# Four attention tiles' sums transposed by VectorE instead of TensorE, in all batches in the same slot

## The reference, cut to what matters

```python
attn_in = jnp.tanh(jnp.einsum('bsd,da->bsa', hidden, W1) + b1)
scores = jnp.einsum('bsa,a->bs', attn_in, v)
mask = where(pt == 0, l <= j, where(pt == 1, l >= j, l != j))   # per batch
p = softmax(where(mask, scores[:, None, :], -1e30), axis=-1)
pooled = einsum('bjl,bld->bjd', p, hidden) / cnt
x = x + pooled
```

## Time and profile before

| what | value |
|---|---|
| median of 3 executions | 500.68 us |
| the profiled execution | 501.22 us |
| its span, first to last instruction | 499.4 us |
| granted TensorE clock, mean | 0.998 |
| PE busy | 493.0 us, 99% of the span |
| DVE busy | 348.8 us, 70% |
| ACT busy | 260.3 us, 52% |
| POOL busy | 236.0 us, 47% |

### The profile page before, as it was taken

The page is one execution under the profiler, slowest core; times in us unless marked ns, Lnnn a source line. Parts: engine busy times, 40 slices in busy tenths (PEclk is TensorE's granted clock), DMA queues, the critical chain, the costliest instruction groups (busy, mean ns, idle before and its releaser), DMA issues.

```text
span 499.4 us, 6992 instructions
## 1 busy us (share of the span) xinstructions
PE 493.0 (99%) x2320; PEld 407.7 (82%) x2320; DVE 348.8 (70%) x702; ACT 260.3 (52%) x506; POOL 236.0 (47%) x201
## 2 busy tenths in 40 slices
PE   8999999999999999999999999999999999999996
PEld 5787888888888888888888888888888888888985
DVE  5587235885688799786478689788568779644467
ACT  4655555543457574444446656454345757445243
POOL 1575446445264446444544447444525444746023
PEclk9999999999999999999999999999999999999999
DMA  5865354322255443422227454422222342331002
GB/s 154 185 185 150 101 147 147 100 85 85 85 120 145 116 115 87 127 85 84 85 85 169 123 161 123 132 84 85 85 85 85 100 112 84 88 131 37 0 1 84
DMA packets 77657, 52.97 MB, mean 106 GB/s; under 512 B 40758, under 2 KB 67382, under 8 KB 77622
## 3 DMA queue, kind: packets, MB, share of 16 engines
q1 hardware_dynamic: 75734, 50.44, 35.5%
q10 hardware_dynamic: 1888, 2.10, 1.3%
HBM read 48.33 MB, written 2.10 MB: 101 GB/s over the span
## 4 chain that ended last, share of the span: by engine, by line
PE 90%; DVE 5%; DMA 3%; issue 1%; ACT 0%; ACTq 0%; DVEq 0%; SPq 0%
PE ps_hid L839 14%; PE ps_hid L840 14%; PE ps_hid L844 14%; PE ps_net L901 13%; PE ps_net L896 13%; PE ps_net L897 13%; DMA raw_wo<-in_L_cond_share_wo_dram 3%; PE ps_net L868 2%; DVE pick L1680 1%; DVE hid_lo L1827 1%; PE ps_side L537 1%; PE ps_side L541 1%; PE ps_side L536 1%; PE ps_side L547 1%; PE ps_side L550 1%
## 5 line engine op out<-in xcount | busy, mean ns | idle before, releaser
L1924 POOL TENSOR_TENSOR wi_lo<-raw_wi,wi_hi 128x512 fp32r<-128x512 f32 x77 | 101.6, 1319 | 207.5 <-ACT wo_hi L1088 110.2
L1109 ACT ACTIVATE hid_hi<-ps_hid 128x512 fp32r<-128x512 f32 x160 | 95.5, 598 | 194.1 <-PE ps_hid L844 192.3
L1827 DVE SCALAR_TENSOR_TENSOR hid_lo<-ps_hid,hid_hi 128x512 fp32r<-128x512 f32 x160 | 109.8, 688 | 113.9 <-ACT hid_hi L1109 112.5
L839 PE MATMUL ps_hid<-x2T_hi,wi_lo 128*128 128x512 f32 (+1 forms) x332 | 125.9, 381 | 0.0
L840 PE MATMUL ps_hid<-x2T_hi,wi_hi 128*128 128x512 f32 (+1 forms) x332 | 125.3, 379 | 0.0
L896 PE MATMUL ps_net<-hid_hi,wo_hi 128*128 128x512 f32 x304 | 118.9, 391 | 0.0
L897 PE MATMUL ps_net<-hid_hi,wo_lo 128*128 128x512 f32 x304 | 118.5, 390 | 0.0
L1925 POOL TENSOR_TENSOR wo_lo<-raw_wo,wo_hi 128x512 fp32r<-128x512 f32 x77 | 104.1, 1352 | 0.0
L844 PE MATMUL ps_hid<-x2T_lo,wi_hi 128*128 128x512 f32 (+1 forms) x332 | 98.9, 379 | 0.0
L901 PE MATMUL ps_net<-hid_lo,wo_hi 128*128 128x512 f32 x304 | 94.0, 390 | 0.3 <-DVE hid_lo L1827 0.3
L839 PEld LDWEIGHTS ps_hid<-x2T_hi,wi_lo 128*128 128x128 f32 x332 | 62.4, 188 | 11.9 <-POOL wo_lo L1925 0.2
(11 more groups left out here) (329 smaller groups left out, 500.1 us busy)
## 6 DMA issues: line engine op xcount, KB each, us to landing
raw_wi<-in_L_cond_share_wi_dram SPq DMA_DIRECT2D x23, 512.0 KB, 3.8
raw_wo<-in_L_cond_share_wo_dram SPq DMA_DIRECT2D x23, 512.0 KB, 4.8
raw_wi<-in_L_cond_expert_wi_dram SPq DMA_DIRECT2D x16, 512.0 KB, 3.8
raw_wo<-in_L_cond_expert_wo_dram SPq DMA_DIRECT2D x16, 512.0 KB, 4.8
next_x2T<-in_x_dram SPq DMA_DIRECT2D x24, 64.0 KB, 4.3
x_rows<-in_x_dram SPq DMA_DIRECT2D x3, 512.0 KB, 4.1
x_rows<-netT SPq DMA_DIRECT2D x48, 32.0 KB, 2.0
out_dram<-out_rows SPq DMA_DIRECT2D x5, 256.0 KB, 5.7
```

The source lines that it names most:

```text
L839: mm(dst, wi_lo[:, w, k, c], x2T_hi[:, k, rows], start=(k == 0), stop=False)
L1109: fn(hid_hi[:, ring(b, q)], ps_hid[:, ring(b, q)], ACT.Relu).then_inc(hid_hi_ready, 1)
L1827: v.scalar_tensor_tensor(out=hid_lo[:, ring(b, q)], in0=ps_hid[:, ring(b, q)], scalar=0.0, in1=f32(hid_hi[:, ring(b, q)]), op0=ALU.max, op ...
L1924: g.tensor_tensor(wi_lo[:, w], raw_wi[:, half % 2, :, c], f32(wi_hi[:, w]), ALU.subtract)
```

## The change

DVE transposes the tile sums. `sum_columns` shrinks to 32 columns per half, of which one copy fills the first four. A wait for that copy is new. Four instructions then transpose 32 partitions x 64 elements each in blocks of 32x32 into `tile_sums`, 32 partitions x 256. PE's two transposes and PE's wait for `sum_columns` go. In slot 20 ACT writes `tsum` by two copies of 32x256 from SBUF, to partition groups 0 and 2, where it copied 128x256 from PSUM; DVE's subtraction reads `tile_sums` and group 0 of `tsum`, both in SBUF, where it read PSUM and SBUF. `LATE_TSUM` goes: batch 2's copy and subtraction stand in slot 20 too. Group 3 of `tsum` is zeroed once at the start.

```diff
-    LATE_TSUM = SLOTS - CH
-        sum_columns = sb("sum_columns", [P, KD, P])
+        sum_columns = sb("sum_columns", [P, KD, G])
+        tile_sums = sb("tile_sums", [G, D])
@@ PE
-                if slot == (LATE_TSUM if i == LATE else C_SLOT["tsum"]):
-                    tile_sums(i)
-            def tile_sums(i):
-
-                pe.wait_ge(c_dve.sem, c_dve.at(i, "sum_columns"))
-                for k in range(KD):
-                    last = nc.tensor.transpose(tsum_bank(False)[:, k * P:(k + 1) * P], sum_columns[:, k], ident[:])
-                last.then_inc(c_pe.sem, 1)
@@ ACT
-                if slot == (LATE_TSUM if i == LATE else C_SLOT["tsum"]):
-                    tile_sums_copy(c_pe, c_act, i, tsum[:, 0:D], False)
+                if slot == C_SLOT["tsum"]:
+                    act.wait_ge(c_dve.sem, c_dve.at(i, "tile_sums"))
+                    fn(tsum[0:G, 0:D], tile_sums[:], ACT.Copy)
+                    fn(tsum[2 * G:3 * G, 0:D], tile_sums[:], ACT.Copy).then_inc(c_act.sem, 1)
@@ DVE, slot 17
-                for k in range(KD):
-                    blocks = sum_columns[:, k].rearrange("p (b g) -> p b g", g=G)[:, 0:3, 0:R]
-                    last = v.tensor_copy(blocks, tile_sums_T[:, k].rearrange("p (o t) -> p o t", o=1).to_broadcast([P, 3, R]))
+                v.tensor_copy(sum_columns[:, :, 0:R], tile_sums_T[:]).then_inc(c_dve.sem, 1)
+                here("sum_columns")
+                for a in range(P // BK):
+                    last = v.transpose(tile_sums[:].rearrange("p (k d) -> p k d", d=P)[:, :, a * BK:(a + 1) * BK], sum_columns[a * BK:(a + 1) * BK])
                 last.then_inc(c_dve.sem, 1)
                 v.tensor_copy(tsum[:, D:VW], tile_den[:]).then_inc(c_dve.sem, 1)
                 here("den_hi")
@@ DVE, slot 20
-                v.tensor_tensor(tsum[G:2 * G, 0:D], tsum_bank(False)[G:2 * G], f32(tsum[G:2 * G, 0:D]), ALU.subtract).then_inc(c_dve.sem, 1)
+                v.tensor_tensor(tsum[G:2 * G, 0:D], tile_sums[:], f32(tsum[0:G, 0:D]), ALU.subtract).then_inc(c_dve.sem, 1)
-                if slot == (LATE_TSUM if i == LATE else C_SLOT["tsum"]):
+                if slot == C_SLOT["tsum"]:
                     split_tile_sums(i)
@@ DVE, start
             v.memset(sum_columns[:], 0.0)
+            v.memset(f32(tsum[3 * G:P]), 0.0)
```

More of the change, by code:

```diff
@@ L288, in cond_resid_program @@
         gate_sum = Steps(sem("gate_added"), "g0k0 g0k1 g1k0 g1k1 g2k0 g2k1 g3k0 g3k1")
-        c_pe = Steps(sem("c_pe"), "gate_row att score_row tsum out0 out1 out2 out3")
+        c_pe = Steps(sem("c_pe"), "gate_row att score_row out0 out1 out2 out3")
         c_act = Steps(sem("c_act"), "gate_exp x3hi0 x3hi1 att_below att tile_exp wgt exp tsum_hi")
         c_dve = Steps(sem("c_dve"), "gate_hi gate_lo gate_scores gate_max gate_rec gates comb00 comb10 comb01 comb11 comb02 comb12 comb03 comb13 x3lo0 x3lo1 row_blocks mask "
-                                    "att_sum att_hi att_lo diag score_col prefix max1 suffix tops top neg_top sel own bias max2 val_hi val_lo arg sums sum_columns den_hi den_lo "
+                                    "att_sum att_hi att_lo diag score_col prefix max1 suffix tops top neg_top sel own bias max2 val_hi val_lo arg sums sum_columns tile_sums den_hi den_lo "
                                     "wgt_hi phi plo wgt_lo tsum_lo den0 rden0 out0 out1 den1 rden1 out2 out3")
@@ L311, in score_banks @@
             return (ps_side[:, 0, HS:S], ps_side[:, 1, 0:HS]) if final else (ps_side[:, 1],)
-        def tsum_bank(final):
-            return ps_net[0:3 * G, 0, 0:VW] if final else ps_side[:, 0, 0:D]
+        tsum_bank = ps_net[0:3 * G, 0, 0:VW]
         def tile_cols(t):
@@ L803, in last_attention @@
                 for t in range(R):
-                    last = mm(tsum_bank(True), edge_diag[:, 3 * G * t:3 * G * (t + 1)], last_values[:, t], start=(t == 0), stop=(t == R - 1))
+                    last = mm(tsum_bank, edge_diag[:, 3 * G * t:3 * G * (t + 1)], last_values[:, t], start=(t == 0), stop=(t == R - 1))
                 last.then_inc(e_pe.sem, 1)
@@ L906, in batch @@
                     first_product(b, q, first, last)
-                    if not first and (not last or q < C_SLOT["out"] or q == LATE_TSUM):
+                    if not first and (not last or q < C_SLOT["out"]):
                         stage_c(q, b - 1)
@@ L1002, in prob_exp, with tile_sums_copy @@
                 return fn(prob[:, f, tile_cols(t)], prob[:, f, tile_cols(t)], ACT.Exp, bias=score_col[:, t:t + 1])
-            def tile_sums_copy(pe_s, act_s, n, dst, final):
-                act.wait_ge(pe_s.sem, pe_s.at(n, "tsum"))
-                fn(dst, tsum_bank(final), ACT.Copy).then_inc(act_s.sem, 1)
+            def tile_sums_copy():
+                act.wait_ge(e_pe.sem, e_pe.at(0, "tsum"))
+                fn(tsum[0:3 * G], tsum_bank, ACT.Copy).then_inc(e_act.sem, 1)
             def gate_hidden():
@@ L1069, in last_probabilities @@
                 probabilities(0)
-                tile_sums_copy(e_pe, e_act, 0, tsum[0:3 * G], True)
+                tile_sums_copy()
                 weights(1)
@@ L1594, in last_attention @@
                 dve.wait_ge(e_act.sem, e_act.at(0, "tsum"))
-                done(v.tensor_tensor(tsum[G:2 * G], tsum_bank(True)[G:2 * G], f32(tsum[G:2 * G]), ALU.subtract))
+                done(v.tensor_tensor(tsum[G:2 * G], tsum_bank[G:2 * G], f32(tsum[G:2 * G]), ALU.subtract))
                 here("late_rden")
```

## The result

The changed kernel takes 504.69 us (median of 6, 503.33 to 504.91) against 500.73 us for the kernel before (6 executions): ratio 1.0070, interval 1.0056 to 1.0084. It is slower, as forecast, by about 4.0 us instead of 1.6; the range ended at 503.1. Two later measurements of the same kernel gave 1.0072 (1.0054 to 1.0091) and 1.0068 (1.0050 to 1.0086), with medians 3.3 and 3.2 us above those of the kernel before beside them; four single traced executions took 503.17 to 504.70 us.

The account below looks back on a forecast made before the run. PE bounds the kernel, working without a break unless hid_lo is late; late hid_lo of slot 18, net of PE's saving, gives 0.53 + 0.53 + 0.60 = 1.66, say 1.6 us: 500.68 + 1.6 = 502.3 us, range 500.0 to 503.1.

Parts of the forecast that it names:

- the first wait: PE at L901 of slot 20 waits for hid_lo of slot 18: 0.41 us later than before in batch 1, restart 0.12 more.
- The 0.60 for four overlapping transposes: DVE's four transposes ahead of the tile_den rounding: 0.60 us if they overlap, 0.92 if each waits for the one before.
- A: The forecast: POOL holds both tile_den steps, hid_lo of slot 18 late by two POOL instructions; 502.3 us, chance 0.65.
- B: Rival, not slower: the two-element rounding L1488 passes POOL, only the subtraction is held, PE never waits; 500.1 us, chance 0.20.
- C: Rival, worse: the transposes are slow or held by POOL too, hid_lo starts at about 189.3; 503.0 us, chance 0.10.
- D: Rival, all hidden: transposes under 0.1 us each, both small steps get in before POOL; 499.9 us, chance 0.05.
- PE's saving: Transposes dropped from PE in slot 20 of batches 1 and 2 and slot 32 of batch 3: 0.29 + 0.29 + 0.22 = 0.80 us.
- Behind it: DVE's steps after hid_lo of slot 18: 0 to 0.25 us a batch, 0 to 0.7 in all, nearly nothing taken.
- A's own range: Range given for the main forecast of 502.3 us: 501.8 to 503.1 us.
- The move of the late batch: Batch 2's copy and subtraction go from slot 32 to 20; PE waits for neither before the very end: nothing.
- ACT's copies: Slot 20: two 32x256 copies replace one of 128x256; ACT has 1.36 us of work in 2.98, so put at nothing.
- The subtraction from SBUF: DVE in slot 20: can hold to a POOL instruction's end; nothing under PE's shift, about 0.1 us without it.

Follow-up runs that it names:

- den_first: Changed kernel with the two small steps on tile_den put ahead of the copy and the transposes: 501.09 us, ratio 1.0004 to the kernel before.
- one_transpose: Changed kernel with only the first of the four DVE transposes, the rest left out: 500.66 us, ratio 0.9994 to the kernel before.
- before_plus4: Kernel before with four spare DVE transposes put behind the copies, all else untouched: 504.01 us, ratio 1.0054; measured again 503.83 us, 1.0054.
- late_slot32: Changed kernel with ACT's copies and DVE's subtraction for late batch 2 in slot 32 of batch 3 again: ratio 1.0070 to the kernel before.
- one_group: Changed kernel with all four transposes reading partitions 0 to 31 of sum_columns: 504.63 us, ratio 1.0064 to the kernel before.

## Why the prediction was wrong

**Right: the mechanism, its place, its size at the first wait.** Rounding and subtraction held to the ends of POOL's pair, 0.69 (0.46 in batch 2) and 1.20 us (about 0.8 to 1.1 and 1.2 forecast; the rounding came late, because the four transposes took 0.97 us and not 0.60 to 0.92); `hid_lo` of slot 18 at 188.90, or 189.07 with the 0.17 that this execution was ahead, against 189.11; PE at L901/L890 late by 0.40 against 0.41, restart 0.10 to 0.12 against 0.12. The 0.60 for four overlapping transposes did not follow from the prediction's own parts (three distances of 0.15 and one duration of 0.23 are 0.68); the hold to POOL's end made that harmless. The three exchanges A is built on (`den_first`, `one_transpose`, `before_plus4`) all went its way (`one_transpose` with no hold where one was expected); B, C and D are out. PE's saving shows as -0.25 in the kernels without the hold and -0.23 at chunk 30.

**Wrong: "Behind it".** The prediction worked out that POOL might be first at `prob_lo`, that L901 of slot 21 would then wait 0.1 us and pay 0.12 again, 0 to 0.25 us a batch, and took "nearly nothing of it, since the shift of PE itself opens the room". POOL was first (190.06 against 190.29), and it cost 0.23, 0.24 and 0.27 us (the steps at chunks 19 and 20 less the first restart): 0.1 of wait and 0.14 of restart, the upper end. That reason was an error: the shift of PE had already been used in the sum (L901 "shifted to about 192.7"). And the race was read as near, 190.23 for DVE against 190.27 for POOL, when it was not: from the end of `hid_lo` of slot 18 to the start of `prob_lo` DVE needed 0.70 us (189.59 to 190.29), the prediction had 0.43 for the two roundings between. POOL's start hangs on ACT's `wo_hi` and moved with nothing on DVE, so DVE lost by 0.23. With that term at its upper end, 0.7 us, the sum is 2.4, near the 2.3 of the trace, and the forecast 503.0. It is the mis-sized term of the sum.

**Wrong: the baseline for the rest.** The remaining 0.9 to 1.7 us of the 3.2 to 4.0 stand in no step of the prediction. It took one traced execution as standing for the median in both kernels. The traced start-up alone spreads over 1.7 us (-0.51 to +1.17, in all kernels), wider than the 1.3 us of A's own range; A's range had no term for it. Beyond that there is the surplus of untraced executions, whose cause is not settled.

**Edits put at nothing.** The move of the late batch: nothing, as said (`late_slot32`). ACT's copies: no step of PE in the traces stands at their place that the two waits do not explain. The subtraction from SBUF: not held in the changed kernel (0.41 us, L1487). In `den_first`, without PE's shift, L1487 came 0.24 us late in slot 22 of two batches; the prediction had about 0.1 (up to 0.2 in B), and it was L1535 ahead of it that was held.

The Trainium skill ("SBUF — State Buffer", section "Who interferes with whom") describes the lock as full blocking of the later of the two engines. The trace agrees for a rounding of two elements per partition (0.69 us, where 0.12 to 0.17 is what it takes free) and for a subtraction of two (1.20 against 0.15).

## What to carry to other kernels

When work is put ahead of a small SBUF-to-SBUF step, look not at the slack of what follows but at when POOL's next instruction starts: 0.12 to 0.17 us turn into 0.5 to 1.2 for each such step, and dependent steps lose one POOL instruction each. Put small steps that can be held first, and steps that read PSUM or transpose (neither was held here) across POOL's work. Having found one new wait, carry the late times on until the engines are back in their old distances: the second wait was worth half of the first, and a term that hangs on which engine comes first by 0.04 us belongs in the sum at its worse end.

## What the runs showed of the hardware

- Four 32x64 transposes that read four partition groups take 0.97 us, about 0.23 each, one behind the other; reading one group, 0.61 (`one_group`).
- Transposes are not held by POOL: the four took 0.97 us across the start of its instruction in three kernels, and one alone ahead of it the same 0.23. Nor is `hid_lo` held, which reads PSUM (0.69 from 187.06 in `den_first`, under POOL's instructions from 186.21 on).
- After a hold ends, the dependent small DVE step is taken up 0.04 us later (187.63 to 187.67) and has already lost to POOL's next instruction, in all three batches. A step that already stands there when POOL's instruction ends goes first: `prob_lo`, taken up at 190.29, ended at 191.95, and the POOL instruction that came next lasted 1.74 us instead of 1.29.
- PE, when it has waited at L890, starts its next product 0.57 us behind it, where 0.46 is usual.
- The time of a traced execution is 501.2 us plus start-up and batches, to 0.05 us; the start-up varies by 1.7 us between traced executions. In the one followed up, the first weights landed late.
